# Second attention on one Trainium2 core: the additions of gathered rows go behind output addition and division in VectorE's order

## What is computed

```python
x = x + _L0_xattn_ref(_layernorm(x), ctx_1024, ctx_1024, ...)
# first experts: the two best of 16 for every row, with weights w
x = x + _L0_ffn_ref(_layernorm(x), ...)
# second attention: 2 heads of 64, keys and values from ctx_1024
def _L1_xattn_ref(x, context, mask, Wq, Wkv, Wo):
    q = (x @ Wq)...; k, v = context @ Wkv
    attn = softmax(where(mask, q k^T * SCALE, -inf))
    return (attn @ v) @ Wo
x = x + _L1_xattn_ref(_layernorm(x), ctx_1024, mask_BxSxS2_bf1, ...)
x = x + _L1_ffn_ref(_layernorm(x), ...)
```

## Time and profile before

| | us |
|---|---|
| median of 3 runs | 1228.61 |
| lowest, highest | 1225.31, 1229.33 |
| the profiled execution | 1240.47 |
| its span, first to last instruction | 1238.8 |
| second attention in it | about 665 to 930 |
| TensorE busy in the span | 917.8 (74%) |
| VectorE busy | 672.8 (54%) |
| ScalarE busy | 586.5 (47%) |
| GpSimd busy | 510.8 (41%) |
| mean granted TensorE clock | 0.865 |

### The profile page before, as it was taken

The page is one execution under the profiler, slowest core; times in us unless marked ns, Lnnn a source line. Parts: engine busy times, 40 slices in busy tenths (PEclk is TensorE's granted clock), DMA queues, the critical chain, the costliest instruction groups (busy, mean ns, idle before and its releaser), DMA issues. The chain is left out here.

```text
span 1238.8 us, 28168 instructions
## 1 busy us (share of the span) xinstructions
PE 917.8 (74%) x9348; PEld 763.5 (62%) x9348; DVE 672.8 (54%) x2254; ACT 586.5 (47%) x1339; POOL 510.8 (41%) x619
## 2 busy tenths in 40 slices
PE   1799696877869640899993367668677798688886
PEld 1578575765757540799993245445456687577775
DVE  4789484755748442544443266667674346234443
ACT  1688484755747310566662245555566341122221
POOL 3011425344242446244435445555300435535555
PEclk9899797978879755899997587997898889989998
DMA  5000101001013203333432122222103113243330
GB/s 172 10 19 16 35 24 39 28 31 34 25 36 124 93 29 115 115 131 131 135 132 79 39 54 63 57 55 61 47 6 124 65 62 146 91 141 108 112 111 28
DMA packets 65775, 90.52 MB, mean 73 GB/s; under 512 B 21997, under 2 KB 45937, under 8 KB 65169
## 3 DMA queue, kind: packets, MB, share of 16 engines
q1 hardware_dynamic: 46576, 48.44, 12.7%
q0 software_dynamic: 17664, 40.41, 10.2%
q10 hardware_dynamic: 1440, 0.43, 0.2%
HBM read 52.64 MB, written 37.63 MB: 73 GB/s over the span
## 5 line engine op out<-in xcount | busy, mean ns | idle before, releaser
L742 POOL DMA_INDIRECT a_got<-f_rows_out,f_pos_i x128 | 120.9, 945 | 108.1 <-DVE x_sb L755 72.9
L1128 POOL DMA_INDIRECT f_rows_in<-f_xn_all,f_pos_i x128 | 125.0, 977 | 82.5 <-DVEq L1189 44.7
L1494 POOL DMA_INDIRECT out<-f1e_y,f1e_ids x80 | 79.9, 998 | 74.7 <-DVE f1e_y L1546 51.5
L604 PE MATMUL a_ps_o<-vx,a_prT 128*64 128x18 f32 x2048 | 92.1, 215 | 19.4 <-issue 18.7
L604 PEld LDWEIGHTS a_ps_o<-vx,a_prT 128*64 128x64 f32 x2048 | 85.5, 139 | 27.7 <-issue 26.4
L1128 POOL DMA_INDIRECT f_rows_in<-f1r_xn_all,f_pos_i x64 | 61.6, 963 | 88.4 <-DVE f1r_xn_all L1362 40.9
L293 POOL TENSOR_TENSOR x_sb<-x_sb,bo 128x256 f32<-128x256 f32 x32 | 23.2, 725 | 180.2 <-DVE a_xn L347 179.9
L590 PE MATMUL a_ps_t<-ident,a_pr 128*128 128x128 f32 x512 | 78.2, 299 | 11.3 <-ACT a_xnT L530 9.2
L1631 PEld LDWEIGHTS f0e_ps_y<-f0e_w,f0e_hT 128*128 128x128 f32 x640 | 83.9, 191 | 4.4 <-ACT f0e_hT L1592 0.2
L1592 ACT ACTIVATE f0e_hT<-f0e_ps_h,f0e_w 128x256 f32<-128x256 f32 x160 | 67.1, 470 | 40.6 <-PE f0e_ps_h L1621 40.6
L1497 POOL DMA_DIRECT2D f_rows_out<-f0e_y x80 | 43.5, 544 | 100.9 <-DVE f0e_y L1549 92.8
(11 more groups left out here) (253 smaller groups left out, 2178.2 us busy)
## 6 DMA issues: line engine op xcount, KB each, us to landing
f1e_x<-f_rows_in SPq DMA_DIRECT2D x40, 272.0 KB
f0e_x<-f_rows_in SPq DMA_DIRECT2D x80, 128.0 KB, 2.0
f_rows_out<-f0e_y POOLq DMA_DIRECT2D x80, 128.0 KB, 2.0
a_ctxT<-in_ctxT SPq DMA_DIRECT2D x64, 128.0 KB, 2.1
f_w<-in_f_w SPq DMA_DIRECT2D x16, 257.0 KB
x_sb<-in_x SPq DMA_DIRECT2D x4, 1024.0 KB
f_w<-in_f_w SPq DMA_DIRECT2D x8, 384.0 KB, 6.7
f_rows_in<-f1r_blank SPq DMA_DIRECT2D x9, 272.0 KB
```

The costliest lines, as they stand in the source:

```text
L604: last = pe.matmul(ps_o[rows, 144 * u + 18 * j:144 * u + 18 * j + 18], prT[:, u, j, rows], vx[:, g, 2 * u + b, j, :, :].rearrange("p e c - ...
L742: pool.indirect_dma_start(got[:, n, k, :], None, N.rows_out, bass.IndirectOffsetOnAxis(ap=N.pos_i[:, k, t:t + 1], axis=0)).then_inc(arrive ...
L1128: pool.indirect_dma_start(N.rows_in, bass.IndirectOffsetOnAxis(ap=N.pos_i[:, k, t:t + 1], axis=0), self.xn_all[:, t, :], None).then_inc(se ...
L1494: pool.indirect_dma_start(rows_of_out, bass.IndirectOffsetOnAxis(ap=ids[:, n, u:u + 1], axis=0), y[:, n, u, :], None, bounds_check=B * S - ...
```

## The change

Only VectorE's order in the bodies of the second attention changes. The first pair of additions of G+3 stands behind the division of G-1; the second pair and the statistics stand behind the statistics of the finished x. No instruction is added or taken away, and no other engine's list changes. Behind the change, lines from L824 on have other numbers (L830 is L828, L837 is L832, L842 is L837, L851 is L846).

```diff
                     if within(G + 2, NG):
                         norm(G + 2, g % 2)
-                    if within(G + AHEAD, NG):
-                        add_result(0, *coming)
                     if within(G - 2, NG):
                         ...
                         dve.tensor_tensor(R.x[:, t, :], ps_y[...], R.x[:, t, :], ALU.add).then_inc(x_done, 1)
-                    if within(G + AHEAD, NG):
-                        for k in range(1, K):
-                            add_result(k, *coming)
                     if within(G - 1, NG):
                         ...  # reciprocal, division
                         last.then_inc(ao_ready, 1)
                     if within(G + AHEAD, NG):
-                        statistics(G + AHEAD, (g + AHEAD) % 2)
+                        add_result(0, *coming)
                     if within(G - 2, NG):
                         ...  # bn_stats of the finished x
                     if within(G + AHEAD, NG):
+                        for k in range(1, K):
+                            add_result(k, *coming)
+                        statistics(G + AHEAD, (g + AHEAD) % 2)
                         aggregate(G + AHEAD, (g + AHEAD) % 2)
```

## The result

The change makes the kernel slower. The kernel before took 1228.97 us in the median of four runs (1225.31 to 1244.2) and the changed one 1261.05 us (1257.08 to 1264.17, four runs): ratio 1.0251, 95% interval 1.0198 to 1.0303. The profiled execution took 1257.08 us, its span is 1255.4 us.

What follows compares the result with a forecast made beforehand. Bound by a loop through four engines: TensorE's results come late while gathers follow one another, so their release is on the path. 25.2 + 3.5 = 28.7 us added to 1228.6 gave 1257 us, range 1225 to 1270.

Steps and rivals of the forecast that it cites:

- What bounds the kernel: Second attention: late TensorE results after gathers close a four-engine loop of 7.07 us a body, gather release on the path.
- Step 1: VectorE's first pair of additions loses its cover, the wait before the output addition, and comes behind the wait for 0.52 us.
- Step 2: Second pair of additions releases the gathers 1.51 us later; 1.4 us a body, 18 bodies, 25.2 us.
- the other case: The output addition's result stays late too, so the whole 1.51 us enters the loop, making it 8.58 us.
- Step 3: Later statistics and aggregation delay ScalarE's L862 and the output projection: 0.5 us in seven bodies, 3.5 us.
- Step 4: Division earlier lets TensorE's L970 start sooner; no gain counted, since L909 stands behind later ScalarE work.
- Rival (a): Gathers' new place lets TensorE's results through, bodies of 5.7 us, 1207 us; chance 0.17.
- Rival (b): Gathers have nothing to do with TensorE's delay; only the later variance costs, 8.9 us, 1238 us; chance 0.13.
- Rival (c): Results get through partway, `o_done` early in half the bodies; mean loop 7.8 us, 1245 us; chance 0.10.
- The prediction's last sentence: The sum is undone if TensorE's delay depends on its work queued during the gathers, not on the gathers' end.

Runs made afterwards that it cites:

- e15: Kernel before with 112 of the second attention's 128 gathers left out, on a chip of the 1239 to 1247 us kind: 1167.81 us, ratio 0.9433.
- e19: Kernel before with 112 of 128 gathers replaced by ordinary DMAs of the same size, on another chip of the slower kind: 1170.36 us, ratio 0.9383.
- e3: Kernel before with 112 of 128 gathers left out, on the chip where the kernel before takes 1062 us: 1060.64 us, ratio 0.9982.
- e9: The changed kernel, unchanged, run again with a profile on a chip of the slower kind: 1266.29 us, ratio 1.0221 against the kernel before.
- e1: Kernel before with both pairs of additions behind the division, statistics left in place, on the 1062 us chip: 1092.20 us, ratio 1.0286.
- e16: Kernel before with both pairs of additions ahead of the output addition, on a chip of the slower kind: 1252.86 us, ratio 1.0098.
- e17: Kernel before with a 0.96 us GpSimd fill ahead of each body's gathers, VectorE untouched, slower kind of chip: 1245.68 us, ratio 1.0029.
- e10: Kernel before with only the second pair of additions behind the division, on a chip of the slower kind: 1244.53 us, ratio 1.0045.
- e18: Kernel before with both pairs of additions behind the division, statistics left in place, on a chip of the slower kind: 1265.52 us, ratio 1.0222.
- e8: The kernel before, unchanged, run again with a profile on a chip of the slower kind: 1234.51 us profiled, 1239.56 us median of 13.
- e4: Kernel before with both pairs of additions ahead of the output addition, on the 1062 us chip: 1063.66 us, ratio 1.0013.
- e2: Kernel before with only the coming group's statistics moved behind those of the finished x, on the 1062 us chip: 1067.99 us, ratio 1.0041.

## Why the prediction was right, point by point

**What bounds the kernel** held: the release of the gathers is on the path, though GpSimd is half idle. What the profile of before could only suggest (the delay goes with the gathers) e15 shows: take them away, and the bodies fall from 7.1 to 5.2 us. The prediction cited the Trainium skill ("SBUF — State Buffer", "Who interferes with whom"), by which a DMA never contends with a compute engine. With that rule the traces agree for ordinary DMAs (e19, bodies of 5.24 us) and on the chip of e3, and they do not for indirect ones on the chips of the first kind (7.1 us). The page speaks of access to SBUF; whether the lateness arises there, no run tells.

**Step 1**, first pair: its cover did go. L828 passes at once, and the first pair stands behind the wait for `o_done`: 0.52 us, in rows from 808.30 to 808.82.

**Step 2** is the second of the prediction's two cases, "L830's result gets through early and only L837's wait on `o_done` stays late", with 8.24 us and perhaps 0.1 more. Measured: 8.11 in the body shown, 8.14 in the mean, 8.24 in e9. Its terms: 2.37 forecast and 2.41 measured from reciprocal to gather, 3.74 and 3.74, 2.12 and 1.96. GpSimd's wait for VectorE is 3.45 us in that body, where "nearly 4" was said. The 1.4 us that was taken a body lay towards the other case (1.5) and was too much; 0.99 us (8.14 less 7.15) is what the 24 bodies lost in the first pair of profiles, 1.15 in the second. The count was too small: all 24 bodies up to 917.61 are held in the changed kernel, not 18. In before six of the 24 were irregular, and short and long ones (5.28, 11.62) summed to the same mean. 24 x 0.99 = 23.6 stands against 25.2; two errors nearly cancelled.

**Step 3**, the later variance, forecast 0.5 us for seven bodies, 3.5 in all. Measured 0.79 (6.01 less 5.22) for two bodies and 2.0 for the third, part of which ran at the lower clock, in sum 3.6: the sum fits, price and count do not. The rows of such a body, which answer to the earlier trace rows:

```profile
917.61 0.71 PE L984 MATMUL a_y<-w1wo,a_aoT 128*128 128x128 f32 x4 [1.46 <-ACT a_aoT L907]
919.43 0.18 DVE L832 RECIPROCAL a_rec<-a_o 128x4 f32<-128x4 f32 x1 [0.51 <-PE a_o L996]
922.35 0.25 DVE L770 BATCH_NORM_AGGREGATE a_mv<-a_comb 128x2 f32<-128x6 f32 x2
922.63 0.29 ACT L860 ACTIVATE a_log_var<-a_mv,eps 128x2 f32<-128x2 f32 x1 [0.68 <-DVE a_mv L770]
923.62 0.71 PE L984 MATMUL a_y<-w1wo,a_aoT 128*128 128x128 f32 x4 [1.82 <-ACT a_aoT L907]
```

L832 starts 1.82 us after L984 (forecast 1.84). L770 ends 4.99 us after it, where the prediction's times give 906.5 - 901.81 = 4.69: the 0.3 us between is what was missing. It was summed as a one-time delay and is a loop of its own, projection to projection in 6.01 us, with no waiting engine in it that could give way. On the chip of e1 it is what the move of the additions costs.

**Step 4**, division earlier, counted as nothing; no gain is to be seen in the changed kernel's rows.

What the sum lacked is the stage's start, 4 to 4.5 us gained, because eight gathers in one train became two trains of four. With it the first pair of profiles reads -4.5 + 23.6 + 3.6 = 22.7 us in the stage, the second -4.1 + 27.6 + 3.0 = 26.5, against 28.7 forecast and a difference of the medians of 32.1 us (24.3 to 37.2 by the interval). So the mechanism was right, and that 1257 lies within 4 us of 1261.05 is in part luck: the price a body was too high, their number too small, the start's gain was not in the sum, and 6 to 9 us of the medians' difference stand in neither pair's stage.

**Rival (a)** named the right moment and lost there. Counted over the semaphore events between 735 and 865 us: in the kernel before, 61 results of TensorE end by the model 3.0 to 5.5 us after the first gather of a train, and all 61 are signalled more than 0.3 us late; of 45 that end in the first 2 us five are. In the changed kernel 41 of 42 that end 3.0 to 5.5 us after the first gather are late, and none of the five that end sooner. The output projection ends 2.5 us after the first gather and passes; attention times v ends at 3.6 us and is held, as the prediction put it ("It decides at the moment of `o_done`"). But the time since the first gather is not the whole rule. In the train of 28 at the stage's start of the kernel before a result that ends 20.2 us after the first gather gets through at once (L868 at 685.75), while the next one waits until 705.04; and in the changed kernel's first train of four one that ends 1.8 us after the first gather is held for 2.4 us (L874 at 716.91). **Rival (b)** falls with e15, on a chip of this kind. On the chip of e1 its premise, that the gathers don't delay TensorE's results, describes what is seen. **Rival (c)**, bodies in which the result comes partway, is seen in a result that does not set the loop: v's gets through 0.3 to 0.5 us after the fourth gather's start in nine of 23 bodies of the changed kernel, and 1.9 us after it in the others. `o_done` never does, and all 24 bodies lie between 8.06 and 8.25 us.

The prediction's last sentence, on what would undo the sum, names what e16 and e17 then showed: where the gathers stand against TensorE's work matters as much as when they end. That the loop's arithmetic came out for e9, e10, e18 and the changed kernel, where `o_done` is the late result that sets the loop in every body, and not for e16 and e17, is the limit of it.

Still open: which part of an indirect DMA holds the results back, why the kinds of chip differ in it, and whether the held results are written late or only signalled late.

## What to carry to other kernels

An engine that is half idle can still be on the path, if what it starts delays what others wait for; compare a body that has this work with one that has not before calling its waits free. Price a moved release by the loop it closes, and look which of the waits in the loop is late last: the price is counted from there. Forecast the size of such a loop only where the same result is late in every body, and test a reorder on more than one chip, because e1 and e18, one kernel on two chips, lose 2.9% and 2.2% for different reasons.

## What the hardware showed that was not expected

- In the first two profiles, and on the chips of e8 to e10 and e16 to e18, TensorE's results come late while indirect DMAs follow one another; for the chip of e19 only the time of before, 1246.86 us, says the same. On the chip of e1 to e4 none of some 500 results of e1, e2 and e4 came more than 0.3 us late during gathers of about the same length (950 to 960 ns) and pitch.
- How long a result is held is not fixed. After a train of four the reciprocal goes on about 2 us after the last gather's start (1.7 to 2.2 us in the changed kernel, e9 and e18); after the 28 at the stage's start ScalarE goes on 5.7 us after it in the kernel before (705.04 less 699.30) and 5.4 us in the changed one.
- The kernel before takes 1239 to 1247 us on the ones and 1062 us on the other. In the 24 bodies the difference is 7.1 against about 5.3 us each (e4, e2), some 44 us; most of the rest lies outside the stage: its first gather starts at 665.5 us in before and at 597.3 us in e4. In the first attention L530, a copy on ScalarE, stands still for 73.4 us until "remote" in the former and in the latter never waits for "remote", so the same delay may be at work there; no run tried it.
- Ordinary DMAs of the same size from the same engine, 537 ns each, hold nothing back (e19), at a higher rate of bytes (78 GB/s against 58).
- The granted clock went with the waits. In the windows of 24 bodies it is 1.00 in e15 and e19, without waits, and 0.81 (e16) to 0.91 (e8) in the held ones; a matmul group of the output projection takes 0.71 us at the full clock and 1.22 at the lower. What this adds to the gathers' cost is not priced apart.
